# Where the causal mask of the row maxima is added in the last attention: a TensorE product or a fused VectorE operation

## The reference

```python
y = jnp.einsum('bse,ef->bsf', x, W1) + b1          # 16 heads of q, k, v with 8 features each
w = jnp.einsum('bhqd,bhkd->bhqk', q, k) / dk
mask = jnp.tril(jnp.ones((S, S)))
w = w * mask - NEG_BIG * (1.0 - mask)              # NEG_BIG = 1e10, S = 1024
w = jax.nn.softmax(w, axis=-1)
attn = jnp.einsum('bhqk,bhkd->bhqd', w, v)
```

## Time and profile before

| | us |
|---|---|
| median of 3 runs | 1888.76 |
| lowest and highest | 1886.09 to 1895.93 |
| the profiled execution | 1889.65 |
| its span | 1887.8 |
| PE busy | 1666.1 (88%) |
| DVE busy | 1331.1 (71%) |
| ACT busy | 1092.2 (58%) |
| POOL busy | 1084.0 (57%) |

### The profile page before, as it was taken

The page is one execution under the profiler, slowest core; times in us unless marked ns, Lnnn a source line. Parts: engine busy times, 40 slices in busy tenths (PEclk is TensorE's granted clock), DMA queues, the critical chain, the costliest instruction groups (busy, mean ns, idle before and its releaser), DMA issues. The chain is left out here.

```text
span 1887.8 us, 33663 instructions
## 1 busy us (share of the span) xinstructions
PE 1666.1 (88%) x12976; PEld 1385.9 (73%) x12976; DVE 1331.1 (71%) x2744; ACT 1092.2 (58%) x2240; POOL 1084.0 (57%) x1029
## 2 busy tenths in 40 slices
PE   5999999999999999989957898955888468999997
PEld 4888888888888888877855777844677355666676
DVE  6888888888788878843453477577677588777782
ACT  3677767767777767655544555622433345666666
POOL 3888899999999999990055454634177410101011
PEclk9999999999999999989978999966999689999999
DMA  3000000000100000000014200030155200000000
GB/s 94 15 1 6 11 1 15 1 15 1 37 1 1 1 1 1 1 29 0 1 60 139 70 11 2 2 95 0 43 143 134 49 1 1 1 2 2 1 2 24
DMA packets 57839, 47.92 MB, mean 25 GB/s; under 512 B 8384, under 2 KB 49504, under 8 KB 57552
## 3 DMA queue, kind: packets, MB, share of 16 engines
q1 hardware_dynamic: 48128, 32.92, 5.8%
q0 software_dynamic: 8496, 12.33, 3.0%
q10 hardware_dynamic: 1056, 0.52, 0.1%
HBM read 36.45 MB, written 9.31 MB: 24 GB/s over the span
## 5 line engine op out<-in xcount | busy, mean ns | idle before, releaser
L750 POOL TENSOR_TENSOR dtl<-dts,dth 128x512 fp32r<-128x512 f32 x256 | 353.3, 1380 | 20.5
L680 DVE TENSOR_REDUCE nm<-PS 128x1 f32<-128x1024 f32 x256 | 311.4, 1217 | 28.3 <-PE PS L200 27.4
L2035 ACT ACTIVATE ET_a<-PS 128x256 f32<-128x256 f32 (+2 forms) x512 | 222.7, 493 | 122.6 <-PE PS L1948 77.8
L748 POOL CAST dth<-dts 128x512 fp32r<-128x512 f32 x256 | 234.8, 917 | 50.6 <-ACT dts L607 49.5
L198 PE MATMUL PS<-xh,yh 128*128 128x512 f32 x512 | 225.2, 440 | 10.4 <-ACT XNT L600 5.3
L1846 POOL TENSOR_SCALAR_AFFINE_SELECT ET_a<-ET_a 128x1024 f32<-128x1024 f32 x32 | 35.0, 1094 | 309.4 <-ACT ET_a L2035 309.4
L141 PE MATMUL PS<-C,XN 128*128 128x128 f32 x1120 | 176.6, 283 | 39.5 <-POOL W4h L1121 24.0
L200 PE MATMUL PS<-xh,yl 128*128 128x512 f32 x512 | 204.0, 399 | 0.0
L199 PE MATMUL PS<-xl,yh 128*128 128x512 f32 x512 | 203.8, 398 | 0.0
L600 ACT ACTIVATE XNT<-PS,nm 128x1024 f32<-128x1024 f32 x128 | 142.8, 1115 | 72.2 <-DVE nm L680 71.3
L607 ACT ACTIVATE dts<-PS 128x512 f32<-128x512 f32 x256 | 152.6, 598 | 46.4 <-POOL dtl L750 44.1
(11 more groups left out here) (430 smaller groups left out, 4386.8 us busy)
## 6 DMA issues: line engine op xcount, KB each, us to landing
e_wg<-in_WgT SPq DMA_DIRECT2D x16, 256.0 KB
e_wu<-in_WuT SPq DMA_DIRECT2D x16, 256.0 KB
e_wd<-in_WdT SPq DMA_DIRECT2D x16, 256.0 KB
m_x_rows<-m_xs SPq DMA_DIRECT2D x1, 1472.0 KB, 5.1
m_xs<-m_x_rows SPq DMA_DIRECT2D x5, 256.0 KB, 4.3
m_y_rows<-m_xs SPq DMA_DIRECT2D x5, 256.0 KB, 2.3
X<-in_L_attn_X SPq DMA_DIRECT2D x2, 512.0 KB, 4.4
wqn<-in_L_attn_Wq SPq DMA_DIRECT2D x8, 128.0 KB, 2.2
```

The lines of the kernel that those rows point to most:

```text
L680: e.tensor_reduce(self.nm[:, half, i:i + 1], self.S[half], AX.X, MAX, negate=True).then_inc(*self.top.up((g, half)))
L748: e.tensor_copy(hi, src).then_inc(*ts.up((g, g4, "h")))
L750: e.tensor_tensor(lo, src, f(hi), SUB).then_inc(*ts.up((g, g4, "l")))
L2035: e.activation(dst, src, ACT.Exp, scale=self.SC, bias=0.0).then_inc(*self.ex.up(it))
```

## The change

In `kind == 3` TensorE no longer issues the mask product. The row product of each part stands alone and sets the signal. For the 8 parts of a head with a diagonal, VectorE's `tensor_reduce` is replaced by `tensor_tensor_reduce`: it reads the scores from PSUM and the mask from SBUF (bf16), adds them, multiplies by -1, writes the result back over the scores in PSUM, and takes the minimum along the row, from an initial value of 3e38. The 4 parts without diagonal keep `tensor_reduce`. `mk` becomes 512 columns wide, with 384 columns of zero ahead of the mask, so that the slice that ends at column 512 fits every width. GpSimd writes the zeros instead of `identb`. The wait for the mask moves from TensorE's queue to VectorE's. Layer 1 is unchanged.

```diff
--- before.py
+++ after.py
@@ -1073,8 +1073,8 @@
         self.WO = sb("WO", [128, 128])
         self.bq, self.bm = sb("bq", [128, 2, 4]), sb("bm", [128, 2, 4])
         self.b2 = sb("b2r", [128, 128])
-        self.identb = sb("identb", [128, 128], BF16)
-        self.mk = sb("mk", [128, 3, 512] if kind == 1 else [128, 1, 128], BF16)
+        self.identb = sb("identb", [128, 128], BF16) if kind == 1 else None
+        self.mk = sb("mk", [128, 3, 512] if kind == 1 else [128, 512], BF16)
         self.VA = sb("VA", [128, NT * 16 * 9 + 32])
         self.va = self.VA[:, 0:NT * 144].rearrange("p (n h c) -> p n h c", n=NT, c=9)
         ea = k.sb(early, "early" + n, [128, 1408])
@@ -1086,7 +1086,7 @@
         for w in range(2):
             ops += [(p, w, g) for g in range(3) for p in "hl"] + [("h", w, 3), ("l", w, 3)]
         ops += ["one"] if kind == 3 else ["bq0", "one"]
-        ops += [("bm", 0), ("bm", 1), "ident"] + ([("mask", i, j) for i in range(3) for j in range(2)] if kind == 1 else ["mask"]) + ["va1", "va0"]
+        ops += [("bm", 0), ("bm", 1)] + (["ident"] + [("mask", i, j) for i in range(3) for j in range(2)] if kind == 1 else ["open", "mask"]) + ["va1", "va0"]
         self.ready = k.sig("s_weights", ops)
         self.ends = []
 
@@ -1133,13 +1133,14 @@
         q.wait_ge(ready, "one")
         for w in range(2):
             e.tensor_scalar(self.bm[:, w, :], self.bq[:, w, :], m3[:, w:w + 1], None, MUL).then_inc(*ready.up(("bm", w)))
-        e.tensor_copy(self.identb[:, :], k.ident).then_inc(*ready.up("ident"))
         if self.kind == 1:
+            e.tensor_copy(self.identb[:, :], k.ident).then_inc(*ready.up("ident"))
             for i, us in enumerate(((128, 64), (64, 64), (64, 0))):
                 for j, u in enumerate(us):
                     e.tensor_copy(self.mk[:, i, 256 * j:256 * j + 256], k.cst("band")[:, u:u + 256]).then_inc(*ready.up(("mask", i, j)))
         else:
-            e.tensor_copy(self.mk[:, 0, 0:128], k.cst("caus")).then_inc(*ready.up("mask"))
+            e.memset(self.mk[:, 0:384], 0.0).then_inc(*ready.up("open"))
+            e.tensor_copy(self.mk[:, 384:512], k.cst("caus")).then_inc(*ready.up("mask"))
         e.memset(self.va[:, :, :, 8:9], 1.0).then_inc(*ready.up("va1"))
         e.memset(self.VA[:, NT * 144:], 0.0).then_inc(*ready.up("va0"))
 
@@ -1918,13 +1919,12 @@
                 q.wait_ge(self.k_act if hh % 2 == 0 else self.k_dve, ("k", n, 1, hh))
                 q.wait_ge(self.mi, ("project", n, 0, 1))
             o = self.bank_free(q, it)
-            q.wait_ge(w.ready, "mask" if self.kind == 3 else ("mask", 2, 1))
+            if self.kind == 1:
+                q.wait_ge(w.ready, ("mask", 2, 1))
             if self.kind == 3:
                 i, c0, c1, first = self.rparts[j]
                 wd = max(c1 - c0, 256)
-                t = e.matmul(o[:, 0:wd], qs[:, 128 * i:128 * i + 128], kh[:, c0:c0 + wd], start=True, stop=first)
-                if not first:
-                    t = e.matmul(o[:, c1 - c0 - 128:c1 - c0], w.identb[:, :], w.mk[:, 0, 0:128], start=False, stop=True)
+                t = e.matmul(o[:, 0:wd], qs[:, 128 * i:128 * i + 128], kh[:, c0:c0 + wd], start=True, stop=True)
             else:
                 e.matmul(o, w.identb[:, :], w.mk[:, (0, 1, 1, 2)[j], :], start=True, stop=False)
                 for i in (2 * j, 2 * j + 1):
@@ -2193,7 +2193,13 @@
             if self.kind == 3:
                 i, c0, c1, first = self.rparts[j]
                 dst = self.P2[:, n % 2, i - 4, hh:hh + 1] if first else M[:, i, col]
-                e.tensor_reduce(dst, o[:, 0:c1 - c0], AX.X, MAX, negate=True).then_inc(*self.top.up(it))
+                if first:
+                    e.tensor_reduce(dst, o[:, 0:c1 - c0], AX.X, MAX, negate=True).then_inc(*self.top.up(it))
+                else:
+                    if j == 0:
+                        q.wait_ge(w.ready, "mask")
+                    e.tensor_tensor_reduce(out=o[:, 0:c1 - c0], in0=o[:, 0:c1 - c0], in1=w.mk[:, 512 - (c1 - c0):512], scale=-1.0,
+                                           scalar=3e38, op0=ADD, op1=MIN, accum_out=dst).then_inc(*self.top.up(it))
                 if j == self.nr - 1:
                     m4 = M[:, 4:8, col].rearrange("p i c -> p (i c)")
                     q.wait_ge(self.top, it)
```

## The result

The changed kernel takes 1883.44 us (median of 7 runs, 1881.73 to 1887.92) against 1892.11 us for the kernel before in the same runs. The ratio is 0.9952, with a 95% interval from 0.9937 to 0.9966. Repeated on two other occasions it was 0.9966 (0.9951 to 0.9981) and 0.9956 (0.9940 to 0.9973). So the gain is real and small, 0.3 to 0.5%, some 5 to 9 us, at the edge of what I had called measurable. I had forecast 14.8, from 1889.65 down to 1874.

A forecast was written before the change was run, and what follows sets the result against it. TensorE bounds the middle stretch, VectorE the rows-alone stretch. -20.0 (masks) + 2.8 (rows alone) + 1.0 (chain) + 1.4 (heads like 16) = -14.8 us from 1889.65 gives 1874.9, 1874 as median; range 1864 to 1890.

The forecast's parts named there:

- The three regimes: Last attention: rows alone (46 us) VectorE busy, TensorE waits; rows and columns (260 us) both busy; columns alone (48 us) unchanged.
- 182 x 0.11 = 20.0 us off: Middle stretch: 182 of 216 mask products lie on the chain of waits, each worth 0.11 us on TensorE.
- about 10.8 and 11.6: Forecast times in us of heads 17 and 18, which contain a projection's way over TensorE, ScalarE and VectorE.
- the first rival: Loop over three engines sets heads 17 and 18, so only heads 15 and 16 gain: 1882 us, chance 0.12.
- rows alone +2.8: First stretch, VectorE is the path: 5 heads x 8 masked maxima x 0.07 us surcharge added.
- The chain's +1.0: Middle stretch: two masked reductions on the chain in each of 7 groups of four heads, 0.07 us each.
- head 16's +1.4: Heads like 16, where VectorE has no room left: 0.2 us given back in each for small hand-over waits.
- The bound of 0.17: Upper surcharge per masked maximum on VectorE: the pair does not overlap its neighbours, losing 0.08 us, plus 0.08 for the read.
- a surcharge of 0.19: Point per masked maximum, in us, from which the third rival decides: VectorE fills heads 15 and 16.
- The second: Rival: surcharge of 0.17 us per masked maximum on VectorE leaves 4 us net gain, 1885 us; chance 0.15.
- The third: Rival: reading scores and writing back to the same PSUM bank take turns, making it slower, 1930 us; chance 0.16.
- The fourth, the clock: Rival: TensorE at 1.2 GHz into the middle stretch costs 3 us, 1877; no own chance, counted in the forecast's 0.57.

The follow-up runs named there:

- x3_act_dve: Changed kernel with half of each exponential's columns and half of each row maximum's width left out; heads like 15 take 7.00 us instead of 7.72.
- e2_none: Changed kernel with the mask left out of the row maxima altogether, plain reductions on VectorE; ratio 0.9960 to the kernel before.
- e3_late: Changed kernel with the mask added by TensorE in heads 0 to 4, by VectorE in heads 5 to 31; ratio 0.9960 to the kernel before.

## Why the prediction was right, and where its size was off

The time lies in the range, and the sign held. The size was too large: 14.8 us forecast, 8.7 by the medians, about 5 within the stage. 1883.44 us lies above the part of the range that I had given to the forecast (1864 to 1879, with 0.57), in the part from 1879 up to which I had given 0.23. And three sizes were off, in part against one another: the gain was half of what I had, the surcharge a third, and the low clock, which was no term of the sum, took nearly half of what was left.

**What bounds the kernel.** The three regimes held. Columns alone stayed at 47 us.

**What is taken away.** The price of a mask product, 0.12 us ahead of another product, holds where nothing else waits: behind a row product a column product of 512 takes 0.23 us (1657.80 to 1658.03 in x3_act_dve). The forecast of 7.25 us for heads like 15 was even too high for TensorE; x3_act_dve has 7.00. The failed step is the multiplication: "182 x 0.11 = 20.0 us off". It took each mask on the chain as a gain in full. Measured, heads like 15 gained 0.40 of 0.88, like 16 0.48 of 0.68, and like 17 and 18 0.29 each, where "about 10.8 and 11.6" meant 0.8 and 0.6. That is 1.46 us in a group, 9.9 in all, with VectorE's surcharge in it, against the 17.6 of -20.0 + 1.0 + 1.4. Without the surcharge, by e2_none, it is 1.58 in a group instead of 2.96, so 10.7 us and not 20.0. From the 9.9 the low clock took some 4.5 back: 2.7 in three heads like 18, and 1.8 in heads 5 and 6, which lost 1.2 us where heads of their kind gained 0.6. That leaves the 5.3 measured.

**What covers it.** The sentence that let this through is "TensorE covers it as long as VectorE has room: head 15 goes to 8.13 - 0.88 = 7.25 us on TensorE against 6.18 + 0.56 = 6.74 on VectorE". It compared sums over a whole head. But rows and columns have three banks each, and a head begins with eight parts before the sums give the other engines a pause. Over these eight parts ScalarE needs 3.39 us and VectorE 3.51, while TensorE without masks can do them in 3.04 (x3_act_dve). So the two consumers set the pace there, within a head in which both have over a microsecond of idle time. In the four later parts, whose rows are wide, VectorE alone does. I had named ScalarE only in the first rival, and for heads 17 and 18 only.

**What is added.** Forecast 0.07 us a maximum, measured 0.035; rows alone +2.8 forecast, +0.8 measured. The +0.8 is made up of five heads: head 3 took 0.28 more, heads 1 and 2 0.2 each, head 4 0.6 more, at a granted clock of 0.62 instead of 0.77, and head 0 0.4 less. In head 0 the first four maxima take 1.76 us instead of 2.22, since TensorE, at the lower clock there in both kernels, no longer makes a mask product ahead of each; e3_late, with the mask products back in these heads, has the 7.11 us of before. The chain's +1.0 and head 16's +1.4 together were about 0.9 by the heads of e2_none, 0.13 in a group. The masked reductions that the chain passes over stand in heads like 18, not like 17: 1670.80 in the earlier trace rows lies in head 14. There are two in a group, as I had counted. The bound of 0.17 adds up to 0.16 by its own terms (0.08 and 0.08), and at a surcharge of 0.19 VectorE would fill head 16 but not head 15 (6.18 + 1.52 = 7.70 of 8.13). Neither changes the forecast.

**The rivals.** The first (only heads like 15 and 16 gain, 1882 us) gave a time near the measured one for a wrong reason: all four kinds gained, each by less. The second (s = 0.17) and the third (the two streams take turns in the bank) are out: the fused operation of 512 columns, in place in PSUM, lasts 699 ns, a plain reduction of that width in the same kernel 686. Of the Trainium skill's page "VectorE: DVE Perf Modes", section "The DRAIN you can't avoid", I had used only the sentence that the next operation waits until the pipe is empty; the same section adds that a next operation which is not held starts earlier. The trace agrees with the addition: the operation at 1561.86 lasts 0.47 us, to 1562.33, and the next one starts at 1562.24. The fourth, the clock, was right for the end of rows alone and what follows: 0.6 us in head 4 and 1.8 in heads 5 and 6, where I had 3. But as much again, 2.7, came in heads like 18 (in the first repeat in heads like 17), where I had seen the idle time and not asked what it would do to the clock once it grew.

## What to carry to other kernels

When an engine at 100% gets work taken away, ask over the shortest loop of buffers who hands them back, and not over the whole period: here three banks and eight parts, in which two engines with idle time elsewhere needed 3.4 and 3.5 us against TensorE's 3.0. To find how many engines stand behind the bound, halve the work of each alone and of all together; one alone may show next to nothing. Work that fills TensorE's gaps in a loop over other engines may be worth its own price in clock, so look at the granted clock by stretch after removing it.

## What the runs showed of the hardware

- A custom two-input VectorE operation with an accumulator, in place in PSUM, costs 0.01 us over a plain reduction of the same width behind a plain one (0.34 us for 256 columns), and 0.05 behind another such pair (0.38 for 256, 0.65 for 512). Its read is listed with 139 ns and begins together with the next operation. The groups of the changed kernel, VectorE (busy us, mean ns):

```profile
L2197 DVE TENSOR_REDUCE P_a<-PS 128x1 f32<-128x512 f32 x96 | 65.9, 686 | 7.6 <-PE PS L1927 7.6
L2201 DVE CUSTOM_DVE_ANT_0 PS<-PS,mk 128x512 f32<-128x512 f32 x64 | 44.7, 699 | 0.0
...
L2201 DVE DVE_READ_ACCUMULATOR2_ANT XNT<- 128x1 f32 x256 | 35.5, 139 | 0.3
```

- A product of 128 columns between two wide ones costs 0.04 us of its own and 0.08 at its successor (1685.51 to 1685.55 and 0.31 instead of 0.23, in the earlier trace rows). A product whose weight load waited for a bank takes longer by about the same, 0.08 to 0.11 us (0.28 instead of 0.17 for 384 columns, 0.31 instead of 0.23 for 512, above).
- TensorE's granted clock fell in 15 of 60 heads like 17 and 18 without mask products (17 took longer), and in 1 of 50 with them, though these products are short work.
